# First score operand issued from three queues, output-bias chain one step later, and late norm turns in other banks, in a gated cross-attention and MoE kernel

## The reference, cut to what matters

```python
x = x + tanh(g_xattn) * attention(layernorm(x), ctx)     # 32 batches, x 112x256, ctx 375x256, 16 heads of 16
x = x + tanh(g_ffn)   * moe(layernorm(x))                # 8 experts, top 2, inner width 352

Q, K, V = q @ Wq + bq, ctx @ Wk + bk, ctx @ Wv + bv
attention = softmax(Q K^T / 4) V @ Wo + bo
moe: weights, experts = top_k(softmax(x @ w_router.T), 2)
     sum over the two of weight * ((silu(x w1) * (x w3)) w2)
```

## Time and profile before

| | |
|---|---|
| median of three runs | 856.07 us |
| profiled execution, its own time | 855.32 us |
| its span | 853.6 us |
| mean granted TensorE clock | 0.991 |
| busy: PE / DVE / ACT / POOL | 825.3 / 486.3 / 422.2 / 476.2 us |
| first matmul of real work | 11.41 us |
| attention steps 0 to 31 | about 42.4 to 571 us |
| expert tiles | about 571 to 844 us |

### The profile page before, as it was taken

The page is one execution under the profiler, slowest core; times in us unless marked ns, Lnnn a source line. Parts: engine busy times, 40 slices in busy tenths (PEclk is TensorE's granted clock), DMA queues, the critical chain, the costliest instruction groups (busy, mean ns, idle before and its releaser), DMA issues.

```text
span 853.6 us, 21453 instructions
## 1 busy us (share of the span) xinstructions
PE 825.3 (97%) x7209; PEld 673.7 (79%) x7209; DVE 486.3 (57%) x1163; ACT 422.2 (49%) x1086; POOL 476.2 (56%) x570
## 2 busy tenths in 40 slices
PE   7899999999999999999999999899999999999995
PEld 6578888888888888888888888777777777777773
DVE  4566776777777776777787777655622222222221
ACT  2256665665666566656665666565222222222221
POOL 6454434454555555555655465455777766656652
PEclk8999999999999999999999999999999999999997
DMA  5876777776676677676656664574444443444432
GB/s 153 207 161 168 204 177 174 180 192 156 161 181 155 158 175 172 148 175 164 170 117 158 150 160 111 146 192 74 57 63 62 70 69 62 63 63 63 63 57 31
DMA packets 99842, 112.29 MB, mean 132 GB/s; under 512 B 29276, under 2 KB 81124, under 8 KB 99736
## 3 DMA queue, kind: packets, MB, share of 16 engines
q1 hardware_dynamic: 79720, 92.48, 45.1%
q0 software_dynamic: 18512, 17.60, 13.5%
q10 hardware_dynamic: 1504, 0.85, 0.5%
HBM read 35.48 MB, written 17.53 MB: 62 GB/s over the span
## 4 chain that ended last, share of the span: by engine, by line
PE 85%; DVE 11%; issue 2%; ACT 1%; DMA 1%; POOLq 0%; DVEq 0%; ACTq 0%
PE ps L1417 18%; PE ps L1173 10%; PE ps L1478 10%; PE ps L1162 9%; PE ps L1145 9%; PE ps L1130 8%; DVE negmax L869 6%; PE ps L1168 5%; PE ps L1273 3%; PE ps L1332 3%; PE ps L1436 2%; PE ps L1361 2%; PE ps L1265 2%; PE ps L1247 1%; DVE xa L854 1%
## 5 line engine op out<-in xcount | busy, mean ns | idle before, releaser
L869 DVE TENSOR_REDUCE negmax<-ps 112x2 f32<-112x750 f32 x256 | 240.1, 940 | 124.3 <-PE ps L1162 122.8
L594 ACT ACTIVATE probs<-ps 125x448 f32<-125x448 f32 x384 | 209.5, 547 | 101.8 <-PE ps L1130 95.6
L389 POOL DMA_DIRECT2D stack<-negmax_t x128 | 68.2, 536 | 228.5 <-ACT negmax_t L645 220.8
L1130 PE MATMUL ps<-stack 97*125 97x224 f32 x768 | 189.1, 328 | 0.9 <-ACT probs L594 0.4
L1130 PEld LDWEIGHTS ps<-stack 97*125 97x125 f32 x768 | 127.4, 188 | 28.1 <-ACT probs L594 1.5
L1162 PE MATMUL ps<-stack 96*112 96x376 f32 x512 | 136.7, 348 | 7.7 <-DVE negmax L869 5.4
L505 POOL DMA_INDIRECT out_dram<-y,idx x63 | 100.5, 1595 | 69.5 <-issue 34.4
L689 ACT ACTIVATE silu<-ps 128x352 f32<-128x352 f32 x63 | 29.3, 465 | 184.4 <-PE ps L1417 184.4
L1081 DVE TENSOR_TENSOR h<-silu,ps 128x352 f32<-128x352 f32 x63 | 32.8, 521 | 144.6 <-PE ps L1417 144.4
L1168 PE MATMUL ps<-wv_sb,ctx_t 128*125 128x256 f32 x384 | 100.0, 382 | 0.4 <-DVE split L859 0.4
L1173 PE MATMUL ps<-ctx_t,wk_sb 128*128 128x375 f32 x256 | 93.7, 489 | 0.7 <-ACT q_raw L654 0.7
(11 more groups left out here) (221 smaller groups left out, 1216.9 us busy)
## 6 DMA issues: line engine op xcount, KB each, us to landing
stack<-split SPq DMA_DIRECT2D x252, 150.0 KB, 2.7
ctx_t<-in_ctx_dram SPq DMA_DIRECT2D x32, 375.0 KB, 3.9
stack<-split SPq DMA_DIRECT2D x127, 94.0 KB, 2.5
stack<-split SPq DMA_DIRECT2D x127, 56.0 KB, 2.1
out_dram<-xa SPq DMA_DIRECT2D x32, 112.0 KB, 3.5
xn_scratch<-xn SPq DMA_DIRECT2D x32, 112.0 KB, 3.3
xa<-in_x_dram SPq DMA_DIRECT2D x7, 448.0 KB, 5.6
w_sb<-in_L_ffn_w_dram SPq DMA_DIRECT2D x16, 176.0 KB, 3.1
```

The costliest lines, as they stand in the source:

```text
L389: gp.dma_start(dst[:, :, SKP + SQ * h:SKP + SQ * h + SQ], negmax_t[4 * h:4 * h + 4, half, :].bitcast(f32)).then_inc(s_nmrow[half][c % NSLO ...
L594: act.activation(probs[:, n % NP, :], ps[0:KW, EXPB + k % 2, 0:4 * SQ], ACT.Exp).then_inc(s_exp, 1)
L869: dve.tensor_reduce(negmax[:, half, :, p4], ps[0:SQ, m1:m2 + 1, 0:SK], axis=AX.X, op=ALU.max, negate=True).then_inc(s_max, 1)
L1130: last = pe.matmul(ps[0:KW, EXPB + k % 2, QW * m:QW * m + QW], stack[:, place_of(b), p, KW * ch:KW * ch + KW], stack[:, place_of(b), p, SK ...
```

## The change

- GpSimd's three fills of ones and the fill of `v_sb` behind them now wait for the first normed batch (`s_xn` 1).
- Of the sixteen DMAs of the first stack SyncE issues eight, GpSimd five and ScalarE three, in a new `stack_first` that ScalarE runs between step -3 and step -2 and that waits for the query parts (`s_qlo`).
- Four turns of the constant stand ahead of the first query projection.
- The bias chain moves from step -1 to step 0, the adds of x(0) and x(1) on GpSimd with it to step 1.
- In steps 29 to 31 the turn of the first half's maxima uses bank BB_ and waits for ScalarE's copy of the other half, not for `s_o_nat`; in step 31 the second half's turn uses bank BC and waits for `s_xn2_t`, not for `s_lg`.
- The last seven list pieces move: the piece from step 27, slot 2 comes in step 26, slot 5; the last is in step 29, slot 1, not slot 5.

```diff
-MAP_AT = [... (9, 5), (11, 2), (11, 5), (12, 2), (12, 5), (13, 1), (13, 2), (13, 5))]
+MAP_AT = [... (9, 5), (10, 5), (11, 1), (11, 2), (11, 5), (12, 2), (12, 5), (13, 1))]
...
-            return 256 * (n // NSLOT + 1) - (96 if n % NSLOT == 0 else 0)
+            return 256 * (n // NSLOT + 1) - (80 if n % NSLOT == 0 else 0)
...
+                    def low_keys(g):
+                        rows, pr = slice(32 * g, 32 * g + 32), slice(DC * g, DC * g + DC)
+                        sp.dma_start(dst[32:64, pr, :], src[rows, :, KLO:KLO + KQ]).then_inc(s_stack[s % NSLOT], 16)
...
                         for g in range(2):
-                            from_low(g)
+                            low_keys(g)
...
             gp.wait_ge(s_split0, 1)
+            gp.wait_ge(s_xn, 1)
             for n in range(NSLOT):
                 gp.memset(stack[ONE_ROW:ONE_ROW + 1, n, :, 0:SKP].bitcast(f32), 1.0).then_inc(s_one, 1)
...
-                gp.dma_start(dst[64:96, pr, :], src[rows, :, KHI:KHI + KQ]).then_inc(s_stack_gp, 16)
...
-                    if c == 1:
-                        gp.wait_ge(s_xn, 1)
+                    if c == 2:
                         gp.wait_ge(s_bog, 1)
-                        gp.tensor_tensor(xrow(0), xrow(0), bo_gated[:, :], ALU.add).then_inc(s_xb, 1)
+                        for n in range(2):
+                            gp.wait_ge(s_xn, n + 1)
+                            gp.tensor_tensor(xrow(n), xrow(n), bo_gated[:, :], ALU.add).then_inc(s_xb, 1)
...
+            def stack_first():
+                src, dst = split[:, 0, :, :].bitcast(f32), stack[:, place_of(0), :, :].bitcast(f32)
+                act.wait_ge(s_qlo, 1)
+                act.wait_ge(s_khi, DC)
+                for g in range(3):
+                    rows, pr = slice(32 * g, 32 * g + 32), slice(DC * g, DC * g + DC)
+                    act.dma_start(dst[64:96, pr, :], src[rows, :, KHI:KHI + KQ]).then_inc(s_stack[0], 16)
+
             for i in range(FIRST, LAST):
                 step(i)
+                if i == FIRST:
+                    stack_first()
...
                         if a == 0:
+                            for n in range(4):
+                                pe.transpose(ps[:, 2, P * n:P * n + P], ident[:, :], ident[:, :])
                             pe.wait_ge(s_wq, 32)
...
-                        if i >= 3:
+                        if i == B - 1:
+                            pe.wait_ge(s_xn2_t, i - 2)
+                        elif i >= 3:
                             pe.wait_ge(s_lg, i - 2)
...
-                            negmax_turn(b, 1, BB_)
+                            negmax_turn(b, 1, BC if i == B - 1 else BB_)
...
-                        if e is not None:
+                        if i >= B - 3:
+                            pe.wait_ge(s_nm_t, 2 * b + 2)
+                        elif e is not None:
                             pe.wait_ge(s_o_nat, e + 1)
...
-                        negmax_turn(c, 0, BA)
+                        negmax_turn(c, 0, BB_ if i >= B - 3 else BA)
...
-                    if k == 7 and i == -1:
+                    if k == 7 and i == 0:
                         pe.wait_ge(s_wr, 16)
-                        pe.wait_ge(s_nm_t, 1)
+                        pe.wait_ge(s_nm_t, 3)
...
-                    if k == 8 and i == -1:
+                    if k == 8 and i == 0:
```

More of the change, by code:

```diff
@@ L166, in flamingo @@
         MAX_IN = (0, 1, 2, 3, 5, 7, 9, 10)
-        MAP_AT = [(GB * SNAP + n, k) for n, k in ((8, 2), (8, 5), (9, 1), (9, 2), (9, 5), (11, 2), (11, 5), (12, 2), (12, 5), (13, 1), (13, 2), (13, 5))]
+        MAP_AT = [(GB * SNAP + n, k) for n, k in ((8, 2), (8, 5), (9, 1), (9, 2), (9, 5), (10, 5), (11, 1), (11, 2), (11, 5), (12, 2), (12, 5), (13, 1))]
         SPARE = 32 * DC + 16 * (B - GB * (SNAP + 1))
@@ L415, in queries @@
                 if a == 2:
-                    gp.wait_ge(s_stack_gp, 96)
+                    gp.wait_ge(s_stack_gp, 80)
                 if a >= 2:
@@ L446, in step @@
                         gather(t)
-                if c is not None and c > 0:
-                    if c == 1:
-                        gp.wait_ge(s_xn, 1)
+                if c is not None and c > 1:
+                    if c == 2:
                         gp.wait_ge(s_bog, 1)
-                        gp.tensor_tensor(xrow(0), xrow(0), bo_gated[:, :], ALU.add).then_inc(s_xb, 1)
+                        for n in range(2):
+                            gp.wait_ge(s_xn, n + 1)
+                            gp.tensor_tensor(xrow(n), xrow(n), bo_gated[:, :], ALU.add).then_inc(s_xb, 1)
                     gp.wait_ge(s_xn, c + 1)
@@ L579, in step @@
                     if k == 1 and b is not None and b > 0:
-                        negmax_out(b, 1, BB_)
+                        negmax_out(b, 1, BC if i == B - 1 else BB_)
                         if i == B - 1:
@@ L583, in step @@
                     if k == 6 and c is not None:
-                        negmax_out(c, 0, BA)
+                        negmax_out(c, 0, BB_ if i >= B - 3 else BA)
                     if k == 10 and r is not None:
@@ L656, in third_batch @@
                 act.wait_ge(s_stack[0], stacked(0))
-                act.wait_ge(s_stack_gp, 96)
+                act.wait_ge(s_stack_gp, 80)
                 for m in range(DC):
@@ L872, in step @@
                         dve.bn_stats(st2[:, :], xrow(e)).then_inc(s_st2, 1)
-                    if k == 5 and i == -1:
+                    if k == 5 and i == 0:
                         dve.wait_ge(s_tanh, 1)
@@ L880, in step @@
                         last.then_inc(s_bvb, 1)
-                    if k == 9 and i == -1:
+                    if k == 9 and i == 0:
                         dve.wait_ge(s_bo_ps, 1)
@@ L1152, in maxes @@
                 if t == 0 and c == 0:
-                    pe.wait_ge(s_stack_gp, 96)
+                    pe.wait_ge(s_stack_gp, 80)
                 if c == B - 1 and t in (3, 4, 5, 6):
@@ L1157, in maxes @@
                         pe.wait_ge(s_nm_t, 2 * B - 2)
+                    if t == 5:
+                        pe.wait_ge(s_nm_t, 2 * B - 1)
                     pe.wait_ge(s_max, 8 * c + t - 1)
@@ L1236, in step @@
                             pe.wait_ge(s_nm_t, 2 * i + 1)
-                            if i == 0:
+                            if i == 1:
                                 pe.wait_ge(s_bog, 1)
@@ L1322, in step @@
                             pe.wait_ge(s_xn2_t, r)
+                            pe.wait_ge(s_nm_t, 2 * B)
                         pe.wait_ge(s_xn2, r + 1)
@@ L1346, in step @@
                         elif b is not None:
-                            pe.wait_ge(s_nm_t, 2 * b + 2)
+                            pe.wait_ge(s_nm_t, 2 * b + 2 if c is None else 2 * c + 1)
                         else:
```

## The result

The change makes the kernel slower: **867.47 us** (866.95 to 869.44, 4 runs) against 856.79 (4 runs of before beside them), ratio 1.014 [1.0105, 1.0174]. The forecast was 859.9 in a range of 855.5 to 863.5. The profiled execution took 867.92 us, span 866.2, mean granted clock 0.986 (before 855.32, 853.6, 0.991), so 12.6 us are to be found in the trace.

The account below looks back on a forecast made before the run. TensorE holds 85% of the chain of waits and VectorE 11%, so the question was when the expert stage begins. 1.8 + 2.2 + 1.2 - 1.35 = +3.85 us on the 856.07 median gives 859.9 us, range 855.5 to 863.5.

Parts of the forecast that it names:

- Parts 1 and 2: Start: held fills delay the first stack 2.1 us; ScalarE's three list issues take 2.0, key copy of batch 1 +2.55 us.
- Part 3: Start: after TensorE idles 4 to 5 us behind batch 1's first key projection, the clock is low; +2.2 us, at most +3.0.
- Rival A: The clock stays high or is back at once, so no +2.2: net +1.65, 857.7 us; chance 0.20.
- rival B: ScalarE stuck in its three list issues, everything 1.8 us later, clock's full price: net +6.45, 862.5 us; chance 0.27.
- Part 4: Bias chain moved: step 0 starts 1.8 us late, waiting for the first half's maxima, and itself takes 1.2 us more.
- Part 5: Last steps: removed TensorE waits in steps 30 and 31 gain 0.5 and 0.85, -1.35 us; step 29 gives 0.

Follow-up runs that it names:

- experiment 5: The changed kernel with the first stack back on two queues instead of three: 866.31 us, ratio 1.0102.
- Experiment 10: The changed kernel with VectorE's bias operations in slot 3 of step 0 and x's third group loaded one step later: 862.57 us, 1.0079.
- experiment 2: The changed kernel with the bias chain back in step -1: 861.99 us, 1.0070.
- experiment 14: All parts of the change, fills split not held, VectorE's bias operations in slot 3, x's third group later, two w2 loads held for the second gather: 854.12 us, 0.9988.
- experiment 9: The changed kernel with VectorE's three bias operations in slot 3 of step 0 instead of slot 5: 866.2 us, 1.0101.
- 13: Experiment 10 plus 68 idle TensorE turns, 42 before batch 1's query projection and 26 before the first exponential: 860.29 us, 1.0044.
- 8: The changed kernel with slot 5's norm pieces ahead of the bias operations on VectorE: 867.85 us, 1.0150.
- experiment 12: The kernel before with last steps' part, four warm turns, split fills, x's third group later, two w2 loads held for the second gather: 852.1 us, 0.9945.
- 15: Experiment 12 plus 26 idle turns ahead of the first exponential: 853.47 us, 0.9977.
- 16: Experiment 12 with x's third group loaded in its old place: 850.3 us, 0.9941.
- 6: The kernel before with the bias chain moved to step 0 alone: 863.15 us, 1.0080.
- 7: The changed kernel with 42 and 26 turns of the constant in TensorE's two idle stretches: 862.92 us, 1.0081.
- 1: The changed kernel without the wait that holds back the fills of ones: 862.63 us, 1.0096.
- 11: The kernel before with the last steps' turns and list pieces, four warm turns, and fills split two and one: 852.9 us, 0.9977.
- 4: The kernel before with only the last steps' turns in other banks and the list pieces sooner: 853.82 us, 0.9973.
- 3: The kernel before with the held fills alone: 859.72 us, 1.0049.

## Why the prediction was wrong

It named the right sign at 0.38 and gave 0.57 to no change; 867.47 lies 4 us above its range. Against its own 3.85 us the trace has 12.6.

**Right: Parts 1 and 2.** The fills' order, 2.1 us later at the stack and 2.55 at the key copy, came within 0.2. The second normed batch, for which nothing was added, was held for 2.37 us by the first fill, against an upper bound of 0.4; that was hidden, since VectorE then waited 2.79 us for ScalarE's key anyway. What the Trainium skill says against the third queue (page "DMA: Bandwidth & Descriptors", section "Issuing engines are not separate DMA queues") is borne out: experiment 5 finds no gain.

**Right in mechanism: Part 3.** The clock fell in the gap forecast, and cost 1.8 for 2.2; the high end of 3.0 was too much. What the part left out is that the same could happen in every new gap. Rival A (clock stays) fell, and rival B: the three issues took 2.02 us, not the 2.4 from which it decides.

**The first failed step, in Part 4:** "Landings nearby take 3.6 to 4.5 us", put down for the lists as if their landing hung on nothing. It hangs on what was issued ahead. The lists shift by 4.6 us and x's load, on SyncE, by 3.3, so that they change places, and the landing grows to 5.3 us; before it took at most 3.55 (from 38.83 to 42.38). Those 1.8 us are most of what lies between the forecast -0.75 and +1.92. The rest, 0.9, is the time to spare that the part gave the lists, "0 to 1.2 us" with the middle taken: they had about none. (The middle of 43.8 and 44.9 is 44.35, not 44.2; that slip is 0.15.) Experiment 10 shows the first half by moving x alone: 3.34 us. The other half of the sentence, that the chain's absence from step -1 is lost to this wait, was right (experiments 2 and 14), and more so than forecast.

**The second, and the largest:** "VectorE's 1.2 us fit its idle slots", so step 0 costs +1.2. It counted microseconds and not neighbours. The profiles split the 6.2 us, step by step from 22.94 down to 16.78. The chain's own work is 1.6 (experiment 14's 18.38 against 16.78 before, both at full clock; so the +1.2 for what was counted was fair). Pushed by 0.8 us, the norm's pieces fall into GpSimd's query and are held up, with VectorE's maxima and then TensorE behind them, and the clock falls at 66: 2.9 (experiment 9). The half clock at the start, behind the wait for the lists, with 0.3 that went with x: 1.65 (experiments 9 and 13). These are profiles, not medians: the 2.9 recurs in them (step 0 is 22.7 to 23.6 us in the change, 5 and 8, and 20.1 and 19.8 in 9 and 10), but experiment 9's median is only 1.3 us lower.
The row that could have told was in the earlier trace rows, the 0.17 that takes 1.52 beside a fill, and I used it only for the start. GpSimd's query in step 0 lay 0.6 us behind the pieces; it should have been asked how far they may move.

**The third, Part 5:** that steps 29 and 30 give 1.3 us, about the 1.35, is in part luck. Both waits of the earlier trace rows lie between the values of batch 29 and those of batch 30, and there only 0.73 us were gained, as TensorE now waited 0.79 us for the last lists, in none of the terms. The other 0.56 came in step 29, put at 0 because "VectorE wasn't in the way of its turn". It was. Timelines of before:

```profile
539.47 0.42 DVE L849 TENSOR_TENSOR o_nat<-ps,rsum 112x256 f32<-112x256 f32 x1
539.95 0.26 PE L1178 MATMUL ps<-ident,negmax 112*8 112x112 f32 x1
```

The turn follows the end of `o_nat` (539.89); after the change it runs at 552.47, ahead of that end (552.61).

What took the gain back is in step 31, where the part didn't look. The second gather shifts by 11.8 us and the two loads by 11.2, and so they change places, as the lists and x do at the start. Eighteen profiles, by the gather's issue against that of the loads, and from the values of batch 30 to those of batch 31:

| gather against the loads | kernels | us |
|---|---|---|
| loads held, 2.8 to 3.1 ahead | 12, 14, 15, 16 | 11.39 to 11.41 |
| 0.20 to 0.67 ahead | before, 6, 7, 8 | 11.40 to 11.41 |
| 0.17 and 0.25 ahead, clock at half in step 31 | 9, 1 | 15.45, 12.49 |
| 0.11 ahead to 0.12 behind | 10, 13, 11, change | 11.96 to 12.88 |
| 0.30 to 0.74 behind | 4, 3, 5, 2 | 12.08 to 14.37 |

Held back, the same tail keeps its gain: from the values of batch 28 to those of batch 31 39.3 us before, 39.2 after, 37.6 in experiment 12. Experiment 4's median gives more than its trace, so the part's own worth without the hold stays uncertain by a microsecond.

**Left open:** what starts the fall of the clock in a particular run. Experiment 12 had it in step 0 behind a wait of 0.7 us, 16 didn't behind 0.21, and 11 varied by 6 us from run to run.

## What to carry to other kernels

Before an operation is moved on VectorE, look at what GpSimd does in the place where it, and everything queued behind it, will stand: 0.8 us of small SBUF operations cost 2.9 us of step 0 here, in the profile of experiment 9, which has them two slots earlier. Small transfers that an engine waits for should be issued ahead of large loads, on whichever queue; check after every shift of a microsecond whether the two have changed places. It happened twice here, with the lists and x at the start and with the gather and the loads at the end, and an explicit wait ended the second in all four kernels that had it. And a step shortened on one path is worth only what the next wait leaves: the chain taken out of step -1 brought the first exponential no sooner in either pair (the change and experiment 2, experiments 14 and 16). Experiment 6 starts step 0 1.4 us sooner than before, but so does experiment 4, whose start is unchanged.

## What the runs showed of the hardware

- **GpSimd's fills and query operations hold up VectorE's work on SBUF until they end.** Operations of 0.15 to 0.47 us took 1.52 and 2.37 us beside a fill, 2.48 and 2.51 beside four query operations in a row, 0.99 beside a fifth; reductions from PSUM kept their 0.94. The Trainium skill, page "SBUF — State Buffer", section "Who interferes with whom", has the rule: one pair of SBUF ports is shared and locked for a whole instruction, for VectorE operations with two SBUF inputs (against GpSimd's reads) or in a two-port mode, and reductions never contend; the trace agrees. It was held over four instructions, though, not one: L751's 2.48 us reach to the end of the fourth of GpSimd's back-to-back operations.
- **Two transfers of 1.8 KB land in 3.3 to 4.1 us, or in 4.9 to 5.9,** by whether x's 448 KB were issued on another queue behind both or ahead of the second of them (fourteen profiles); the 7.1 us of the gather issued 0.12 us behind the first of two loads of 1.8 MB look like the same thing. The Trainium skill, page "DMA: Bandwidth & Descriptors", section "Queues, rings and completion order", says that the semaphore's write lands only after every earlier write of that DMA engine, across its queues; the table of experiment 10 agrees with it as to x.
- **The granted clock fell to 1.2 GHz again and again behind gaps of a few microseconds** (22, 46 and 66 us in the changed kernel). Turns put into the gaps took two of the three falls away in experiment 7, and the values of batch 0 came 2.95 us sooner. In 13 and 15 it fell all the same, at 38 and 33 us, with no gap of TensorE over 0.7 us in the nine before.
